# The second router's logits computed with the gate weights as stationary operand in quarters of the columns, and the score transpose six parts later

## The reference, cut to what matters

```python
def _L1_ffn_ref(x, gate_w, expert_bias, shared_w1, shared_w2, routed_w1, routed_w2):   # gate_w: 512 x 7
    flat_x = x.reshape(T, D)                                   # T = 4096 tokens, D = 512
    shared_sum = jax.vmap(_ffn, in_axes=(None, 0, 0))(flat_x, shared_w1, shared_w2).sum(0)
    gate_logits = flat_x @ gate_w + expert_bias
    aff = jax.nn.sigmoid(gate_logits)
    _, topk_idx = jax.lax.top_k(aff, TOP_K)                    # 2 of 7 experts for each token
    mask = (topk_idx[:, :, None] == jnp.arange(E_r)[None, None, :]).any(axis=1)
    score = jnp.where(mask, aff, -1.0).T
    _, sel_idx = jax.lax.top_k(score, capacity)                # 585 tokens for each expert
    ...
    out = jax.vmap(_ffn)(inp, routed_w1, routed_w2)
    routed_sum = jnp.zeros_like(flat_x).at[sel_idx].add(out * w[:, :, None])
    return (shared_sum + routed_sum).reshape(B, S, D)
```

## Time and profile before

| | |
|---|---|
| median of 3 runs | 2239.58 us (2237.45 to 2242.8) |
| profiled execution, its own time | 2234.09 us |
| its span | 2232.4 us |
| PE busy | 2082.1 us (93%), 14310 matmul records |
| DVE, ACT, POOL busy | 1408.4, 764.3, 591.1 us |
| convolution stage, 1443 to 1859 us | PE busy 378.19 us, mean granted clock 0.96 |
| 1859 to 2043 us (shared expert) | PE busy 162.37 us, mean granted clock 0.91 |
| 2043 to 2232 us (routed experts) | PE busy 164.59 us, mean granted clock 0.95 |

### The profile page before, as it was taken

The page is one execution under the profiler, slowest core; times in us unless marked ns, Lnnn a source line. Parts: engine busy times, 40 slices in busy tenths (PEclk is TensorE's granted clock), DMA queues, the critical chain, the costliest instruction groups (busy, mean ns, idle before and its releaser), DMA issues. The chain is left out here.

```text
span 2232.4 us, 35922 instructions
## 1 busy us (share of the span) xinstructions
PE 2082.1 (93%) x14310; PEld 1808.5 (81%) x14310; DVE 1408.4 (63%) x2787; ACT 764.3 (34%) x1452; POOL 591.1 (26%) x443
## 2 busy tenths in 40 slices
PE   5899999999999999889999999789988987988997
PEld 3788888888888888879999999667677776767886
DVE  4567677777777776555555555368876775774663
ACT  2333333333333333222222222144554434222332
POOL 1222222222222222100000000067665640002453
PEclk7579999999999999999999999899999996999999
DMA  2211111111111110512222222353444434224565
GB/s 77 73 42 49 48 48 48 48 48 48 48 48 48 48 48 29 170 48 86 101 98 95 95 102 79 127 189 110 153 149 126 150 121 153 90 99 170 144 163 77
DMA packets 107400, 206.30 MB, mean 92 GB/s; under 512 B 13986, under 2 KB 34530, under 8 KB 106210
## 3 DMA queue, kind: packets, MB, share of 16 engines
q1 hardware_dynamic: 99842, 186.91, 24.9%
q0 software_dynamic: 7392, 17.11, 3.7%
HBM read 127.72 MB, written 76.34 MB: 91 GB/s over the span
## 5 line engine op out<-in xcount | busy, mean ns | idle before, releaser
L1301 PE MATMUL psum<-kv,toep 128*128 128x288 f32 x1280 | 324.2, 415 | 42.4 <-ACT yx L1349 25.9
L1301 PEld LDWEIGHTS psum<-kv,toep 128*128 128x128 f32 x1280 | 246.4, 194 | 117.5 <-ACT yx L1349 32.0
L981 POOL TENSOR_SCALAR_AFFINE_SELECT operands<-operands 128x512 f32<-128x512 f32 x128 | 83.6, 653 | 603.0 <-ACT operands L731 602.7
L162 PE MATMUL psum<-xn_t_h,w_gate_h 128*128 128x256 f32 x768 | 232.4, 303 | 1.8 <-DVE x_all L316 1.8
L162 PE MATMUL psum<-xn_t_h,w_up_h 128*128 128x256 f32 x768 | 217.7, 284 | 0.0
L163 PE MATMUL psum<-xn_t_l,w_up_h 128*128 128x256 f32 x768 | 217.7, 283 | 0.0
L164 PE MATMUL psum<-xn_t_h,w_gate_l 128*128 128x256 f32 x768 | 217.6, 283 | 0.0
L163 PE MATMUL psum<-xn_t_l,w_gate_h 128*128 128x256 f32 x768 | 217.4, 283 | 0.0
L164 PE MATMUL psum<-xn_t_h,w_up_l 128*128 128x256 f32 x768 | 216.9, 282 | 0.0
L637 PE MATMUL psum<-operands 128*128 128x33 f32 x1536 | 211.7, 292 | 0.0
L637 PEld LDWEIGHTS psum<-operands 128*128 128x128 f32 x1536 | 197.2, 205 | 16.8 <-issue 5.8
(11 more groups left out here) (295 smaller groups left out, 4922.5 us busy)
## 6 DMA issues: line engine op xcount, KB each, us to landing
toep<-ssm_padded_scratch SPq DMA_DIRECT2D x64, 256.0 KB, 3.5
kx<-in_ctx_pairs SPq DMA_DIRECT2D x32, 384.0 KB, 4.2
x_scratch<-x_all SPq DMA_DIRECT2D x21, 512.0 KB, 2.8
x_all<-in_x SPq DMA_DIRECT2D x16, 512.0 KB, 3.9
operands<-in_ctx_t SPq DMA_DIRECT2D x16, 512.0 KB, 4.8
xn_t_scratch<-xn_t_h SPq DMA_DIRECT2D x16, 512.0 KB, 2.7
xn_t_scratch<-xn_t_l SPq DMA_DIRECT2D x16, 512.0 KB, 3.6
xn_t_h<-xn_t_scratch SPq DMA_DIRECT2D x16, 512.0 KB, 3.7
```

The source lines that it names most:

```text
L162: pe.run.matmul(out, lhs[0], rhs[0], start=first, stop=False)
L981: pool.run.affine_select(out=diag, in_=diag, compare_op=ALU.is_ge, fill=0.0, base=0, pattern=[[0, 2], [0, 2], [1, P]], channel_multiplier= ...
L1301: ins = pe.run.matmul(out, w[:, (o - k) * P:(o - k + 1) * P], pairs, start=(k == 0), stop=(k == o))
```

## The change

The logits of a block of four tiles become four matmuls instead of 16: quarter k of the contraction has its weights, padded from 7 to 32 columns with zeros, as the stationary operand in columns 32k to 32k+31 of the array (`tile_position`), and streams 512 token columns. The result is 128 x 512 in one bank: four partial sums of the logits, transposed. ACT copies it to SBUF (`lgt`). A new turn "sums" then adds the four parts and turns them back: four matmuls with 128 columns of `lgt` as stationary operand and 7 columns of `stack` streaming, a matrix that has a one wherever row and column agree modulo 32. DVE makes `stack` and zeroes the padding at the start of the stage. In the convolution stage "turn" moves one unit earlier, and "sums" takes a turn, and so a bank set, of its own. In the last stage the logits of four tiles go together. `links` gets five more entries ahead of the first count: the score transpose stands behind part 6 instead of part 1, and everything behind it is five parts later. SP no longer waits for the logits ahead of the loads of x3.

```diff
+        gw = sbuf(late, "gw", [P, KT, KCOLS])
+        lgt = sbuf(late, "lgt", [P, BLK * P])
+        stack = sbuf(late, "stack", [P, KCOLS])
         eb = sbuf(late, "eb", [P, ER])
+        gate_zeroed = signal("gate_zeroed")
         gate_loaded = signal("gate_loaded")
...
-                if n >= 36 and n % 8 in (6, 7) and n < 52:
-                    turns.append((("turn", "logits")[n % 8 - 6], (n - 36) // 8))
-            turns += [("turn", 2), ("turn", 3), ("logits", 2), ("tiles", 6), ("tiles", 7), ("logits", 3), ("turn", 4), ("turn", 5),
-                      ("logits", 4), ("logits", 5)]
+                if n >= 36 and n % 8 in (5, 6, 7) and n < 52:
+                    turns.append((("turn", "logits", "sums")[n % 8 - 5], (n - 36) // 8))
+            turns += [("turn", 2), ("turn", 3), ("logits", 2), ("tiles", 6), ("tiles", 7), ("sums", 2), ("logits", 3), ("turn", 4),
+                      ("sums", 3), ("turn", 5), ("logits", 4), ("logits", 5), ("sums", 4), ("sums", 5)]
             set_of = {turn: i % 2 for i, turn in enumerate(turns)}
...
-                        pe.wait_ge({"tiles": tiles_added, "turn": rows_turned, "logits": logits_read}[old[0]], old[1] + 1)
+                        pe.wait_ge({"tiles": tiles_added, "turn": rows_turned, "logits": logits_copied,
+                                    "sums": logits_read}[old[0]], old[1] + 1)
                     if kind == "unit":
...
                         pe.wait_ge(gate_loaded, 32)
+                        for k in range(KT):
+                            at_ = k * KCOLS
+                            ins = pe.run.matmul(bank_t[set_of[turn] * KT][at_:at_ + KCOLS, :].rearrange("p (j c) -> p j c", j=BLK),
+                                                gw[:, k, :], rows[:, n * BLK:(n + 1) * BLK, k * P:(k + 1) * P],
+                                                start=True, stop=True, tile_position=(0, at_))
+                        ins.then_inc(logits_made, 1)
+                    elif kind == "sums":
+                        pe.wait_ge(logits_copied, n + 1)
                         for j in range(BLK):
-                            for k in range(KT):
-                                ins = pe.run.matmul(bank_t[set_of[turn] * KT][:, j * ER:(j + 1) * ER],
-                                                    rows[:, n * BLK + j, k * P:(k + 1) * P], gw[:, k, :],
-                                                    start=(k == 0), stop=(k == KT - 1))
-                        ins.then_inc(logits_made, 1)
+                            ins = pe.run.matmul(bank_t[set_of[turn] * KT][:, j * ER:(j + 1) * ER], lgt[:, j * P:(j + 1) * P],
+                                                stack[:, 0:ER], start=True, stop=True)
+                        ins.then_inc(logits_summed, 1)
                     else:
...
+                    elif kind == "logits":
+                        act.wait_ge(logits_made, n + 1)
+                        act.wait_ge(logits_summed, n)
+                        act.run.copy(lgt[:, :], bank_t[set_of[turn] * KT]).then_inc(logits_copied, 1)
                 for r in range(HT, TILES):
                     normalise(r)
 
             def vector_convolution():
                 dve.run.memset(fill[:, :], 0.0).then_inc(fill_zeroed, 1)
+                dve.run.tensor_reduce(stack[:, :], ident[:, :].rearrange("p (k e) -> p e k", k=KT), AX, ALU.add)
+                dve.run.memset(gw[:, :, :], 0.0).then_inc(gate_zeroed, 1)
 
                 def near_terms(n):
                     g = n // 2
...
+                    elif kind == "sums":
+                        dve.wait_ge(logits_summed, n + 1)
...
-                        sp.run.dma_start(gw[:, :, :], io["gate_w"].rearrange("(k p) n -> p k n", p=P)).then_inc(gate_loaded, 16)
+                        sp.wait_ge(gate_zeroed, 1)
+                        sp.run.dma_start(gw[:, :, 0:ER], io["gate_w"].rearrange("(k p) n -> p k n", p=P)).then_inc(gate_loaded, 16)
...
+            links = [([("affinity", 1), ("rank", SEEN // 8)], []), ([("mask",)], [])] + [([], [])] * 4 + [([], [("score_turn",)])]
             links += [([("count", i)], [("total", i)]) for i in range(len(BITS))]
             links += [([("final",)], [("final_total",)]), ([("choose",)], [("place",)]), ([("number",)], [("slots_turn",)]),
                       ([("slots",)], [])]
...
-                if i + BLK < TOKT:
-                    order.append(("turn", i + BLK))
-                order.append(("logits", i))
+                if j < BLK:
+                    order.append(("turn", SEEN + BLK + j))
+                if j % BLK == 0:
+                    order.append(("logits", j // BLK))
                 if j < PIECES:
                     order.append(("weights", 0, j))
                 order.append(("split", j))
+                if j % BLK == BLK - 1:
+                    order.append(("sums", j // BLK))
             order += [("rank", c) for c in range(SEEN // 8)]
 
...
+                elif name == "logits":
+                    banks.plan((name, *at), 7)
+                elif name == "sums" and at[0] == 0:
                     banks.plan((name,), 6)
                 elif name in ("score_turn", "total", "final_total", "place", "slots_turn"):
...
-                        i = at[0]
-                        j = i - SEEN
-                        bank, filled, emptied, n = banks.at("turn", i)
+                        i = SEEN + at[0] * BLK
+                        for j in range(BLK):
+                            bank, filled, emptied, n = banks.at("turn", i + j)
+                            pe.wait_ge(emptied, n + 1)
+                        bank, filled, emptied, n = banks.at(name, *at)
+                        pe.wait_ge(emptied, n)
+                        for k in range(KT):
+                            at_ = k * KCOLS
+                            ins = pe.run.matmul(bank_t[bank][at_:at_ + KCOLS, :].rearrange("p (j c) -> p j c", j=BLK), gw[:, k, :],
+                                                rows[:, i:i + BLK, k * P:(k + 1) * P], start=True, stop=True,
+                                                tile_position=(0, at_))
+                        ins.then_inc(filled, 1)
+                    elif name == "sums":
+                        bank, filled, emptied, n = banks.at("logits", *at)
                         pe.wait_ge(emptied, n + 1)
                         bank, filled, emptied, n = banks.at(name)
                         pe.wait_ge(emptied, n)
-                        for k in range(KT):
-                            ins = pe.run.matmul(bank_t[bank][:, j * ER:(j + 1) * ER], turned(i)[:, k, :], gw[:, k, :],
-                                                start=(k == 0), stop=(k == KT - 1))
-                        if i == TOKT - 1:
+                        for j in range(BLK):
+                            c = (at[0] * BLK + j) * ER
+                            ins = pe.run.matmul(bank_t[bank][:, c:c + ER], lgt[:, j * P:(j + 1) * P], stack[:, 0:ER],
+                                                start=True, stop=True)
+                        if at[0]:
                             ins.then_inc(filled, 1)
+                        else:
+                            ins.then_inc(sums_part, 1)
...
+                    elif name == "logits":
+                        bank, filled, emptied, n = banks.at(name, *at)
+                        act.wait_ge(filled, n + 1)
+                        act.wait_ge(sums_part, at[0])
+                        act.run.copy(lgt[:, :], bank_t[bank]).then_inc(emptied, 1)
                     elif name == "weights":
...
                         sp.wait_ge(split_low, (blk + 1) * BLK)
-                        bank, filled, emptied, n = banks.at("logits")
-                        sp.wait_ge(filled, n + 1)
                         sp.wait_ge(x3_loaded[blk % 2], 16 * (blk // 2))
```

More of the change, by code:

```diff
@@ L1656, in build_program @@
             table_part = signal("table_part")
+            sums_part = signal("sums_part")
             ids_ready = signal("ids_ready")
@@ L2006, in vector_late @@
                         if at[0]:
-                            bank, filled, emptied, n = banks.at("logits")
+                            bank, filled, emptied, n = banks.at("sums")
                             dve.wait_ge(filled, n + 1)
```

11 lines of the change are left out of this document (4 added, 7 removed).

## The result

The changed kernel takes 2249.85 us (median of 10 runs), the kernel before, run beside it, 2237.78 us: ratio 1.0055, interval 1.0039 to 1.0071. A second set of runs gave 1.0040 (1.0025 to 1.0054). It is slower by 8 to 12 us, where I had forecast 5.0: the sign and the range held, the size was half of what came. The profiled execution of after takes 2252.36 us with a span of 2250.6.

The account below looks back on a forecast made before the run. PE, busy for 93% of the span, was read for where it stands. Terms 4.7 + 5.3 - 5.5 + 0.5 = +5.0 us, on a median of 2239.6, gave 2244.6 us; 8-in-10 range 2236.5 to 2253.

Parts of the forecast that it names:

- Term 1: Convolution stage, two blocks of logits between units: gaps of 3.45 us, one clock loss a block kept; +4.7 us.
- Term 2: End of the convolution stage: later turn copies and ACT's logits copies delay the normalisation and the stage's end; +5.3 us.
- Term 3: Opening of the last stage: ACT's copy of block 7's logits makes DVE's chain slide by 1.4 us.
- Term 4: Score transpose behind part 6: 30 matmuls fill 7.0 us of the 10.8 us wait; gain 5.5 us with the slide.
- Term 5: Last stage behind the transpose, five parts later: routing tail meets other neighbours; +0.5 us, bounds -0.6 and +2.5.
- (a): Rival, new logits products: the column quarters run one after another; +13 us, 2252.6 us; chance 0.15.
- (b): Rival, PE's clock in the convolution stage and opening: fewer 1.2 GHz stretches, not slower; -1.3 us, 2238.3 us; chance 0.27.
- (c): Rival, score transpose: the wait does not close because something else feeds DVE's chain; +7 us more; chance 0.03.

Follow-up runs that it names:

- the filled ones: Changed kernel with 8 products of ident by ident, results unused, behind the logits and the sums of blocks 0 and 1: ratio 1.0015.
- normalised apart: Changed kernel with ACT normalising block 6 right behind turn 4 and block 7 right behind turn 5: ratio 1.0001.
- both edits: Changed kernel with unused products in the waits of blocks 0 and 1, and blocks 6 and 7 normalised behind turns 4 and 5: ratio 0.9975.

## Why the prediction was right in sign and short in size

**Term 1, two blocks between the units (forecast +4.7, bounds 1.4 to 8.0): the term that was sized too small.** The gaps are right: 3.3 to 3.4 us forecast as 3.45, and going back to the old logits here takes 4.9 us off the last column of the table (2128.3 to 2123.4), the 4.7 of the forecast. What failed is the sentence "so I keep one such loss a block". The trace of after has five in the two blocks, that of before two. From unit 38's old place to the first set of 60 records behind the sums, the first block takes 24.45 us (1667.60 to 1692.05) against 18.43, the second 22.40 against 18.47: +6.0 and +3.9, together +9.9, of which 3 x 1.69 us is the clock. This pair overstates it, though: the profile of before is the one with the least loss of five. By the means of the table above the two blocks grew from 71.1 to 78.4 us, +7.3: 4.9 of gaps and 2.4 of clock, just inside my upper bound. I had read off one profile that a wait of 3.13 us leaves the clock alone and taken the number of losses over unchanged. Both readings were too narrow: of ten such waits of 3.1 to 3.5 us behind the turn, in six profiles with the old turns, six were followed by a slow unit. The new order has three waits a block, and the filled ones show that the waits behind the logits and the sums are what costs there.

**Term 2, the end of the stage (forecast +5.3, bounds 2.9 to 9).** Right in the trace: the turn of block 2, the first behind the last units, stands 21.7 us later in the profile of after (below), and the normalisation and the first transfer 26.7 us later: +5.0. From that turn to the transfer, the five profiles with the old turns take 37.8 to 39.4 us, the three with the new ones 44.4 to 45.7: +6.0 on the means. Also right was the cause, ACT's two copies ahead of the normalisation: taken apart, the transfer comes 5.2 us sooner. I had not seen that the sums of block 5 stand 1.9 us behind it as the next thing to end the stage.

```profile
1819.61 1.91 PE L1307 MATMUL psum<-ident,rows 128*128 128x128 f32 x16
```

```profile
1841.30 1.91 PE L1314 MATMUL psum<-ident,rows 128*128 128x128 f32 x16
```

**Terms 1 and 2 together** were 10.0 us. The convolution stage is 415.8, 418.5, 421.1, 416.2 and 418.6 us long in the five profiles with the old turns, 430.0, 430.6 and 430.3 in the three with the new ones: +12.3 on the means. Of the 2.3 us above the forecast, the clock of the units, which term 1 left out, is 2.4; the sum of the two terms' own means, 13.3, is 1 us above the stage's.

**Term 3, the opening (slide +1.4).** The stretch to the transpose is 32.2 to 33.3 us long in the profiles of the old logits and 32.7, 33.6 and 34.7 with the new: a slide of about 1 us, of the forecast's size and not above the scatter. The first hidden product starts 16.7 us after the first transfer before, 16.0 in after and 16.8 and 18.0 in two other profiles, about as forecast.

**Term 4, the transpose (gain 7.0, 5.5 with the slide, where 7.0 less 1.4 is 5.6; "it cannot be more than 7.0").** The wait closed to 5.4 us as forecast. The gain alone was 7.6 and 8.9 us, and transpose to gather fell by 9.6 us on the means (133.4 to 123.8). The 30 matmuls give 7.0 of it. Where the rest comes from is open. The granted clock in the 100 us behind the transpose is 0.94 in both profiles of before, 0.98 and 0.97 in those of after, and 0.97 and 1.00 with the transpose alone; four hundredths of 100 us are up to 4 us of work. But the logits alone, with the transpose where it was and a wait of 11.8 us there, have 0.98 too and still take 132.4 us to the gather. So the higher clock needs no shorter wait, and with the clock alone the stretch was 1 us shorter. The sentence that excluded more than 7.0 did not weigh any of this.

**Term 5 (+0.5)** is below what these runs resolve: the waits for the hidden product's low half and the rows are 1.8 and 1.7 us at the longest, and the table's are short, as forecast. The rows of these two and of the table (L1876, L1861) sum to 7.3 us in after; the same four sum to 6.8 in before.

**Rivals.** (a) fell: eight records of 512 columns in 1.07 us (1.94 at the low clock) are four quarters side by side, where 3.5 us would have been in sequence. By the Trainium skill, "TensorE: Matmul & The Clock Gate", Part 3, my estimate was 1.1 to 1.5 us for four column tiles; the trace is at or below its lower end. The drain on a switch of mode that "TensorEngine Tiling", Key Properties, of the Trainium skill states is small here: the waits behind the logits (2.27 us) and behind the sums (2.48 us) are those that the copies explain. A unit at the full clock takes 5.05 us up to the start of the new logits (1732.24 to 1737.29) and 4.95 up to that of the old ones, so a switch to column quarters cost at most 0.1 us there. (b) fell too, and the other way round: the clock went against the new logits, by 2.4 us in the two blocks. It had the right lever: with the waits filled and the blocks normalised apart the kernel is faster than before. (c) fell with the 5.4 us.

**The sum.** Forecast +5.0; by the profiles' parts, means against means, the convolution stage +12.3, the opening +1.2, the table -9.6: +3.9, and the medians say +8 to +12. The 4 to 8 us between are, as far as profiles tell, in parts that the change leaves alone: in the same profiles the first part is 3.8 us longer on the means. The first part varies from 1443.2 to 1446.3 us over the five profiles of the old turns and from 1443.3 to 1455.7 over the nine with new ones; the last, from first gather to end, from 202.4 to 209.2 without a pattern by kernel (207.8 and 203.2 in two profiles of one kernel, where the wait for the first gathered rows was 5.3 us once and 2.0 us once). Whether the new code pushes the early part up on average, or single profiles mislead, is open: a profile for each run would tell, one for each kernel doesn't. The 5.6 us of clock that normalising apart brings is open in the same way.

**The best version.** The transpose alone has 0.9966 and 0.9960, the changed kernel with both edits 0.9975 and 0.9973 (transpose one part later). In the set that they share the intervals overlap, so neither is shown to be better; the one line does as well as the rest together.

## What to carry to other kernels

Between alternating buffer sets the number of inserted turns is the price, not their content, as long as that is shorter than the spacing (3.4 us here): a product made three times shorter but split in two turns cost 2.4 us more a block. Where an engine's clock is throttled, count the waits that an order of work creates and not only their sum, and price each at what the next unit can lose (1.7 us, in three of four places here), read from several profiles and not from one; work whose result nobody reads can buy it back. And a change of two halves should be timed by halves: one was worth -8 us and the other cost 17.

## What the runs showed of the hardware that I had not expected

- Four fp32 matmuls of 32 columns of weights each, in the four quarters of the columns, end eight records of 512 columns in 1.06 to 1.07 us, where two records in sequence would take 0.88 us and eight 3.5 (0.44 us each by the rate of the 288-column records). Ahead of them the unit took 0.1 us more than ahead of other work.
- Behind 1 us of logits or sums and a wait of 2.3 to 2.5 us, the next work ran partly at 1.2 GHz in seven of eight places in the two profiles of after and in eight of twelve in three others (a unit in 6.81 us in place of 5.12). Behind the old turns' waits of 3.1 to 3.5 us it was six of ten, with units of up to 8.18 us. With 2.05 us of products in the waits, none of twelve did.
- Code that is the same in two executions differs by 12 us over 1443 us (1443.3 and 1455.7), with single stretches at the low clock that are in the one and not in the other.
